# A decoder layer's opening stage: SyncE gets an ordered list, x gets five buffers, and ScalarE takes the first norm's variances

## The chip, the cores and the metric

The kernel runs on one core of a Trainium2 chip. The metric is the time of one execution on the device in microseconds; the time given for a kernel is the median of its runs.

## The reference

A decoder layer with three post-norm blocks over x of 8 batches, 256 tokens and 512 features (B, S, D). `LN` is a layer norm without gain and bias.

```
# 1: linear attention, head width 128 (M: 128x128, z: 128, a scalar gate)
q, k, v = x @ w_q.T, x @ w_k.T, x @ w_v.T;  sq, sk = elu(q)+1, elu(k)+1
mem   = (sq @ M) / (sq @ z + eps)
local = (sum over s' <= s of (sq[s] . sk[s']) v[s']) / (same sum of sq[s] . sk[s'] + eps)
x1 = LN(x + (g * mem + (1 - g) * local) @ w_o.T),   g = sigmoid(gate)
# 2: ctx is k and v, x1 is q; per 8x8 head a causal convolution over 512 features
kv[i,j] = k[i] * v[j];  y = conv(kv[i,j], ssm_kernel[h]) + D[h] * kv[i,j]
x2 = LN(x1 + sum over i of y[i,j] * q[i])
# 3: gated FFN (width 1408) with 4-bit weights and a scale per group of 128
h = silu(x2 @ Wg.T) * (x2 @ Wu.T);  f = h @ Wd.T
out = LN(x2 + f / rms(f))
```

## The kernel before

**Two parts.** `first_stage` is everything up to the first group; `periods` is the regular part. Blocks 2 and 3 go in 8 groups g of 32 tokens of every batch (256 rows of x). In period `it` the engines do the convolution of group `it` and, beside it, the FFN of group `it - 1`. Period 1 and all of block 1 (the attention) and of the conversion of the weights are one opening, written out by hand: each engine walks a list, `START_PE`, `START_DVE`, `START_ACT`, `START_POOL`. A step with `+` belongs to period 1, one without to the first stage. Then come period 2, a loop over periods 3 to 6, period 7 and a last FFN, each by the fixed lists `PE_ORDER`, `DVE_ORDER`, `ACT_ORDER`, `POOL_ORDER` and their `LAST_` forms. Engines meet only at semaphores, and each engine takes its steps strictly in the order of its list; so a step that waits holds up all that stand behind it.

**The attention** goes over 8 slots i of two batches by 128 tokens: slots 0 to 3 hold tokens 0 to 127, slots 4 to 7 tokens 128 to 255. So groups 0 to 3 read only slots 0 to 3. One slot, by the steps' names (PE steps are capital letters): the x rows land in `ring[i % 3]`; `Xa Xb` transpose them, `xa xb` (ScalarE) keep them; `Q` and `V` project, `re` (ScalarE) and `sg` (VectorE) make elu+1, `vk` keeps v; `S` scores, `mk` masks, `M` and `N` fill `p_n0`, `p_n1`, `dn` inverts the denominators, `lc` (ScalarE) and `o` (VectorE) combine, `T` transposes, `ok` keeps, `Oa Ob` project into `p_n0`, `p_n1`, and `ra rb` add x, in place in the ring buffer. Then `bn` (`statistics`: bn_stats and bn_aggr per half, and adding eps, on VectorE), `pw` (GpSimd, power -1/2), `nb` (VectorE, the shift -mean * rs), `nm` (ScalarE, two Identity activations in place), and SyncE stores the slot to `x1_rows` in HBM. A buffer is loaded anew only after its store has landed.

**The weights.** `u0` to `u4` (VectorE) unpack 4-bit codes, `ws0` to `ws32` (GpSimd) scale them, `w` (PE) transposes, `wh` (ScalarE) and `wl` (VectorE) keep high and low halves. `sk` writes the convolution kernel into `kpad`.

**The convolution.** `rv` (ScalarE, `reverse_ctx`) reads the context rows in `cnat[p]`, `f` or `+ct` (PE) transposes them, `kt` keeps, `pr` (GpSimd) makes products, `hk` (ScalarE) and `kl` (VectorE) split them, `c0` to `c15` convolve with the Toeplitz tiles `toe[p]`, `tm` multiplies by q, `tr` sums, `q`/`+qt` transposes q from `xq[p]`, `kq` keeps it, `rt`, `bq`, `pq`, `nq`, `xt`, `xh`, `xl` finish x2. A `+d0` is the convolution step 0 of the next group. In the FFN `g3_1` is tile 3, scale group 1, of gate and up; `rs3_1` (ScalarE) rescales the sum before `g3_2` may go on; `gu`, `hh`, `hl` make h; `y0_5` is tile 5 of the down projection of row half 0; `n0`, `a0`, `b0`, `e0` end a half. `tl` touches Silu, so that its table is loaded.

**SyncE** issues every DMA, on one queue. Its order before is program text, not a list: the weights and x slots 0 to 2, the Toeplitz rows written and read back, then for each slot its store and the load three slots on, with other loads after stores 3 to 6. Period 1's loads (`body(1, late=False)`) follow the last of the stores:

```
        for i in range(SLOTS):
            store_x1(i)
            if i + 3 < SLOTS:
                load_x(i + 3)
```

`ACT_ORDER`, which is not changed, opens each period with `rv0 tl rs0_1`: the reversal of the context rows of the next group, then the first rescale.

Of the kernel before, what the change touches and what calls it, by code (L numbers as in the profile page):

```python
# [12 lines left out]
P = 128  # L13
# [13 lines left out]
GT = 2  # L27
# [8 lines left out]

LATE = ("y1", "n1", "a1", "b1", "e1")
# [278 lines left out]
def first_stage(nc, sb, sem, keep, cv, bank, x, ctx_in, wq, wk, wv, wo, gate, M, z, ssm, ssm_d, gu_packed, gu_scales,  # L316
# [31 lines left out]
    ring = [sb(f"ring{k}", [P, 2, D], F32) for k in range(3)]  # L348
# [23 lines left out]
    in_x = [sem(f"in_x{k}") for k in range(3)]  # L372
    x1_stored = [sem(f"x1_stored{k}") for k in range(3)]
# [11 lines left out]
    o_flipped, oT_kept, proj_done, z_made = sem("o_flipped"), sem("oT_kept"), sem("proj_done"), sem("z_made")  # L385
    stats, rs_made, shifted, x1_made = sem("stats"), sem("rs_made"), sem("shifted"), sem("x1_made")
# [15 lines left out]
    def on_sync(sp):  # L402
        rows = bass.AP(toeplitz_rows.tensor, 0, [[4 * 640, 16], [1, P], [640, 4], [1, D]])

        def load_x(i):
            wait(sp, x1_stored[i % 3], 16 * (i // 3))
            sp.dma_start(ring[i % 3][:], tokens(x, i)).then_inc(in_x[i % 3], 16)

        def store_x1(i):
            sp.wait_ge(x1_made, 2 * i + 2)  # L410
            sp.dma_start(tokens(x1_rows, i), ring[i % 3][:]).then_inc(x1_stored[i % 3], 16)
# [31 lines left out]
        sp.wait_ge(kernel_split, 4)  # L443
        sp.dma_start(toeplitz_rows, kpad[:]).then_inc(rows_stored, 16)
        for p in range(2):
            sp.wait_ge(cv.ctx_reversed, p + 1)
            load_ctx(1, p)
        sp.wait_ge(rows_stored, 16)
        sp.wait_ge(wts_flipped, 4)
        for p in range(2):  # L450
            load_toe(0, p)
        for i in range(SLOTS):
            store_x1(i)
            if i + 3 < SLOTS:
                load_x(i + 3)
            if i == 3:

                sp.wait_ge(x1_stored[0], 32)
                for k in (1, 2):
                    sp.wait_ge(x1_stored[k], 16)  # L460
                for p in range(2):
                    load_rows(cv.xq, cv.in_xq, 0, p)
                for p in range(2):
                    load_rows(cv.xr, cv.in_xr, 0, p)
            if i == 4:
                sp.wait_ge(cv.ctx_reversed, 3)
# [12 lines left out]
        for k in range(3):
            sp.wait_ge(x1_stored[k], 16 * ((SLOTS - 1 - k) // 3 + 1))  # L480

    def on_pool(pool):
# [59 lines left out]
    def on_scalar(act):  # L542
# [105 lines left out]
    def on_vector(dve):  # L648
# [126 lines left out]
        def residual(i, e):  # L775
            dve.wait_ge(proj_done, 2 * i + e + 1)
            r = ring[i % 3][:, e, :]
            nc.vector.tensor_tensor(r, (p_n0, p_n1)[e][:], r, ALU.add).then_inc(z_made, 1)

        def statistics(i):  # L780
            for e in range(2):
                dve.wait_ge(z_made, 2 * i + e + 1)
                nc.vector.bn_stats(st[:, i, e, :], ring[i % 3][:, e, :]).then_inc(stats, 1)
            for e in range(2):
                dve.wait_ge(stats, i * 5 + e + 1)
                dve.sem_inc(cv.seen, 1)
# [16 lines left out]
        def step(s):  # L803
# [47 lines left out]
    def on_tensor(pe, flips):  # L851
# [20 lines left out]
        def flip_x(i, half):  # L872
            pe.wait_ge(in_x[i % 3], 16 * (i // 3 + 1))
# [3 lines left out]
            for k in range(2):  # L877
                for e in range(2):
                    done = flip(p_x[:, (k * 2 + e) * P:(k * 2 + e + 1) * P],
                                ring[i % 3][:, e, (2 * half + k) * P:(2 * half + k + 1) * P])  # L880
# [119 lines left out]
    free = [(sq_made, SLOTS), (xT_kept, 2 * SLOTS), (oT_kept, SLOTS), (z_made, 2 * SLOTS)]  # L1000
# [3 lines left out]
def periods(nc, sb, sem, keep, cv, bank, free, ctx_in, toeplitz_rows, x1_rows, out):  # L1004
# [30 lines left out]
    def on_sync(sp):  # L1035
# [34 lines left out]
        body(1, late=False)  # L1070
# [44 lines left out]
    def on_scalar(act):  # L1115
# [65 lines left out]
    def on_vector(dve):  # L1181
# [134 lines left out]
def decoder_layer(nc, x, ctx_2048, w_q, w_k, w_v, w_o, gate, M, z, ssm_kernel, ssm_d, gu_packed, gu_scales,  # L1316
# [3 lines left out]
    START_PE = ("iw0 Xa0 iw1 iz0 iw2 Xb0 iw3 Q0 V0 Xa1 S0 w0 M0 w1 f0 Xb1 w2 N0 w3 Q1 w4 T0 Xa2 w5 Oa0 w6 Ob0 f1 w7 "  # L1320
# [148 lines left out]
```

## Time and profile before

| what | value |
|---|---|
| median of 3 runs | 579.14 us (578.35 to 579.87) |
| the profiled execution | 574.02 us, span 572.3 us from first to last instruction |
| busy share of the span | PE 92%, ScalarE 72%, VectorE 67%, GpSimd 68% |
| mean granted TensorE clock | 0.984 of 2.4 GHz |

Rows give start and length in us. An engine's idle time stands in brackets, with what ended it; "issue" is idle time for which the profile shows no releaser. PE instructions overlap, so a row's length is longer than its distance to the next row. `PEld` is the weight load. `SPq` is SyncE's issue of a DMA: its length is that of the issue, not of the transfer. Lines are those of the kernel printed above.

### The profile page before, as it was taken

What the parts mean: (1) busy time and instruction counts of PE and PEld (TensorE: products, weight loads), DVE (VectorE), ACT (ScalarE), POOL (GpSimd) and SP (SyncE); (2) the same over time, 40 slices, a digit from 0 to 9 for tenths busy, and PEclk for the clock granted to TensorE, in tenths of its full rate; (3) what the DMA queues carried; (4) which work ended last, traced back from release to release, by engine and by line L of the source; (5) the groups of instructions that cost most, each with busy time, mean ns of one, the idle gap of its engine ahead of it and who ended that gap; (6) DMA issues with size and microseconds to landing.
All of it is one profiled execution on the core that took longest, in us unless ns stands there. A gap on an engine that the chain in (4) does not pass through costs nothing.

```text
span 572.3 us, 11933 instructions
## 1 busy us (share of the span) xinstructions
PE 526.1 (92%) x3798; PEld 396.7 (69%) x3798; DVE 383.4 (67%) x1153; ACT 414.4 (72%) x978; POOL 388.8 (68%) x449
## 2 busy tenths in 40 slices
PE   5897997996999799999999999999999999998992
PEld 4686785875777467767876777687678767765660
DVE  3984665877776457787777768767877777763223
ACT  3474672535789568878897898788778968887980
POOL 2896762596287538976996798499769967972231
PEclk9998998999999899999999999999999999999997
DMA  9214233403022513012210311040121102001001
GB/s 234 74 52 140 74 115 107 129 1 92 2 75 88 133 50 98 3 57 77 89 47 11 110 55 55 20 145 0 55 81 65 37 0 75 2 1 37 2 19 37
DMA packets 26594, 36.44 MB, mean 64 GB/s; under 512 B 4474, under 2 KB 13818, under 8 KB 26554
## 3 DMA queue, kind: packets, MB, share of 16 engines
q1 hardware_dynamic: 26554, 35.94, 20.8%
q8 instruction: 21, 0.34, 0.3%
q14 instruction: 19, 0.16, 0.1%
HBM read 27.46 MB, written 8.47 MB: 63 GB/s over the span
## 4 chain that ended last, share of the span: by engine, by line
PE 78%; ACT 6%; DVE 6%; DMA 4%; issue 4%; SPq 1%; POOL 1%; POOLq 0%; DVEq 0%; ACTq 0%
PE p_cv L141 7%; PE p_cv L143 7%; PE p_cv L142 7%; PE p_n L1277 6%; PE p_n L1279 6%; PE p_n L1278 6%; PE p_qk L1264 5%; PE p_qk L1266 5%; PE p_x L1264 5%; PE p_ct L99 4%; PE p_x L1266 4%; PE p_s L1266 3%; PE p_s L1264 3%; PE p_qk L890 3%; DMA x_rows<-ring 2%
## 5 line engine op out<-in xcount | busy, mean ns | idle before, releaser
L1122 ACT ACTIVATE p_qk<-p_qk,rescale 128x256 f32<-128x256 f32 x192 | 78.7, 454 | 27.5 <-PE p_qk L1266 27.2
L141 PE MATMUL p_cv<-kv_hi,toe 128*128 128x288 f16 x320 | 92.0, 287 | 6.5 <-issue 6.5
L143 PE MATMUL p_cv<-kv_hi,toe 128*128 128x288 f16 x320 | 92.1, 288 | 0.0
L142 PE MATMUL p_cv<-kv_lo,toe 128*128 128x288 f16 x320 | 92.0, 287 | 0.0
L1090 POOL TENSOR_TENSOR h_lo<-w,h_hi 128x256 f16<-128x256 f32 x88 | 59.4, 682 | 45.2 <-ACT h_hi L1139 44.6
L300 POOL TENSOR_TENSOR shared<-shared 128x1024 f32<-128x1024 f32 x32 | 75.5, 2360 | 16.7 <-DVE shared L260 16.6
L1122 ACT ACTIVATE p_x<-p_x,rescale 128x256 f32<-128x256 f32 x192 | 79.0, 458 | 6.2 <-PE p_x L1266 5.5
L1264 PE MATMUL p_qk<-x_hi,wg_hi 128*128 128x256 f16 x256 | 63.0, 273 | 6.3 <-ACT p_qk L1122 3.3
L226 DVE TENSOR_TENSOR kv_lo<-kv,kv_hi 128x1152 f16<-128x1152 f32 x32 | 60.5, 1889 | 11.6 <-ACT kv_hi L190 10.8
L1277 PE MATMUL p_n<-wd_hi,h_hi 128*128 128x512 f16 x176 | 67.0, 381 | 0.5 <-POOL h_lo L1090 0.5
L1278 PE MATMUL p_n<-wd_lo,h_hi 128*128 128x512 f16 x176 | 67.0, 380 | 0.0
L1279 PE MATMUL p_n<-wd_hi,h_lo 128*128 128x512 f16 x176 | 67.0, 380 | 0.0
L242 DVE TENSOR_TENSOR shared<-p_cv,qv 128x128 f32<-128x128 f32 x128 | 36.5, 285 | 44.3 <-PE p_cv L143 44.3
L1264 PE MATMUL p_x<-x_hi,wg_hi 128*128 128x256 f16 x256 | 63.1, 273 | 1.0 <-ACT p_x L1122 0.6
L1266 PE MATMUL p_x<-x_lo,wg_hi 128*128 128x256 f16 x256 | 62.9, 273 | 0.0
L1266 PE MATMUL p_qk<-x_lo,wg_hi 128*128 128x256 f16 x256 | 62.9, 273 | 0.0
L1122 ACT ACTIVATE p_s<-p_s,rescale 128x256 f32<-128x256 f32 x144 | 59.4, 461 | 2.7 <-PE p_s L1266 2.3
L207 POOL TENSOR_TENSOR kv<-kT 128x512 f32<-128x512 f32 x32 | 40.8, 1276 | 26.1 <-DVE kv_lo L226 26.1
L245 DVE TENSOR_TENSOR shared<-p_cv,qv 128x128 f32<-128x128 f32 x128 | 49.6, 388 | 0.0
L302 POOL TENSOR_TENSOR shared<-shared 128x512 f32<-128x512 f32 x32 | 47.9, 1497 | 2.5
L1266 PE MATMUL p_s<-x_lo,wg_hi 128*128 128x256 f16 x192 | 47.5, 274 | 0.0
L1264 PE MATMUL p_s<-x_hi,wg_hi 128*128 128x256 f16 x192 | 47.5, 274 | 0.0
(162 smaller groups left out, 1300.0 us busy)
## 6 DMA issues: line engine op xcount, KB each, us to landing
toe<-toeplitz_rows SPq DMA_DIRECT2D x16, 512.0 KB, 3.7
ring<-in_x SPq DMA_DIRECT2D x8, 512.0 KB, 3.8
cnat<-in_ctx SPq DMA_DIRECT2D x16, 256.0 KB
x_rows<-ring SPq DMA_DIRECT2D x8, 512.0 KB, 2.8
xq<-x_rows SPq DMA_DIRECT2D x16, 256.0 KB
xr<-x_rows SPq DMA_DIRECT2D x16, 256.0 KB
out_x<-fin SPq DMA_DIRECT2D x16, 256.0 KB
shared<-in_L_ffn_gate_up_packed SPq DMA_DIRECT2D x1, 704.0 KB, 6.9
```

Of the source, the lines that this page charges most:

```text
L141: nc.tensor.matmul(dst, hi, kh, start=(mb == 0), stop=False)
L142: nc.tensor.matmul(dst, hi, kl, start=False, stop=False)
L143: done = nc.tensor.matmul(dst, lo, kh, start=False, stop=(mb == lb))
L226: nc.vector.tensor_tensor(cv.kv_lo[h % 2][:], cv.kv32[:], cv.kv_hi[h % 2][:], ALU.subtract).then_inc(cv.kv_low, 1)
L300: nc.gpsimd.tensor_tensor(T[:, :, 0:256], T[:, :, 0:256], T[:, :, 256:512], ALU.add).then_inc(cv.tree, 1)
L1090: nc.gpsimd.tensor_tensor(h_lo[:, i, :], h32[:, i % 2, :], h_hi[:, i, :], ALU.subtract).then_inc(h_low, 1)
L1122: done = nc.scalar.activation(sums, sums, ACT.Copy, scale=rescale[:, p - 1, part * GI + i:part * GI + i + 1])
L1264: nc.tensor.matmul(dst, whi, cv.x2_hi[:, k, :], start=(k == 0 and part == 0), stop=False, skip_group_check=True)
L1266: done = nc.tensor.matmul(dst, whi, cv.x2_lo[:, k, :], start=False, stop=True, skip_group_check=True)
L1277: nc.tensor.matmul(p_y[t][:], h_hi[:, i, c], wd_hi[:, i, :], start=(i == 0), stop=False)
L1278: nc.tensor.matmul(p_y[t][:], h_hi[:, i, c], wd_lo[:, i, :], start=False, stop=False)
L1279: done = nc.tensor.matmul(p_y[t][:], h_lo[:, i, c], wd_hi[:, i, :], start=False, stop=(i == GI - 1))
```

## The change

SyncE gets a list of its own, `START_SYNC`, for what follows the load of x slot 2, and period 1's loads are in it. `x3` loads slot 3, `st0` stores slot 0, `tw` writes the Toeplitz rows, `toe4` loads Toeplitz tile p = 0 of group 2 (number = 2g + p), `cx6` the context rows of group 3, p = 0, and `xq`, `xr` likewise. x gets five buffers, the two new ones being `z3` and `fin`, which the FFN uses from group 0 on; `sq` becomes scratch of the attention too. `bn_stats` and `bn_aggr` go from the attention: `ra rb` now also sum a row (`accum_out`), `bm` makes the negative mean, `qs` (ScalarE, two Square activations with bias and `accum_out`) sums the squared deviations, `bn` scales and adds eps, and `nb` multiplies. The four other opening lists are new orders. The order of the regular periods is not touched.

```
-    ring = [sb(f"ring{k}", [P, 2, D], F32) for k in range(3)]
+    ring = [sb(f"ring{k}", [P, 2, D], F32) for k in range(3)] + [keep["z3"], keep["fin"]]
...
-            pool.wait_ge(stats, i * 5 + 5)
+            pool.wait_ge(stats, i + 1)
...
+        def deviations(i):
+            act.wait_ge(mean_made, i + 1)
+            for e in range(2):
+                nc.scalar.activation(sq[:, e], ring[i % RING][:, e, :], ACT.Square, bias=negmean[:, i, e:e + 1],
+                                     accum_out=dev[:, i, e:e + 1]).then_inc(deviated, 1)
...
-            nc.vector.tensor_tensor(r, (p_n0, p_n1)[e][:], r, ALU.add).then_inc(z_made, 1)
-
-        def statistics(i):
...
+            nc.vector.scalar_tensor_tensor(out=r, in0=(p_n0, p_n1)[e][:], scalar=1.0, in1=r, op0=ALU.mult, op1=ALU.add,
+                                           accum_out=total[:, i, e:e + 1]).then_inc(z_made, 1)
...
-        body(1, late=False)
+        store(0, 0)
...
+    START_SYNC = ("cx2 x3 x4 st0 x5 tw0 st1 x6 st2 st3 toe0 xq0 xr0 xq1 xq2 cx3 xr1 toe1 toe2 cx5 x7 st4 xq4 xq3 cx4 "
+                  "toe3 xr2 xr3 toe4 xq5 st5 toe5 st6 st7 cx7 cx6").split()
-    START_PE = ("iw0 Xa0 iw1 iz0 iw2 Xb0 iw3 Q0 V0 Xa1 S0 w0 M0 w1 f0 Xb1 w2 N0 w3 Q1 w4 T0 Xa2 w5 Oa0 w6 Ob0 f1 w7 "
+    START_PE = ("Xa0 iw0 Xb0 iw1 iw2 iw3 iz0 Q0 V0 Xa1 S0 M0 N0 Xb1 Q1 w0 T0 f0 w1 Oa0 Ob0 w2 w3 S1 Xa2 w4 V1 w5 Xb2 "
+                "M1 N1 Q2 T1 w6 w7 Oa1 Ob1 Xa3 w8 V2 w9 S2 M2 Xb3 N2 w10 w11 Q3 T2 f1 w12 w13 Oa2 Ob2 Xa4 w14 w15 V3 "
...
+                "w28 Xa6 Oa4 Ob4 w29 w30 V5 w31 w32 q0 S5 M5 c0 Xb6 c1 q1 c2 c3 N5 c4 Q6 c5 c6 T5 c7 Oa5 f2 c8 Ob5 c9 "
+                "S6 c10 c11 f3 V6 c12 c13 Xa7 M6 rt0 c14 Xb7 c15 q2 N6 Q7 +c0 q3 T6 +c1 rt1 Oa6 Ob6 +c2 xt0 V7 xt1 S7 "
...
+                "+g10_2 +d1 +y0_6 +g10_3 +xt0 +y0_7 +y0_8 +y0_9 +xt1 +y0_10").split()
-    START_DVE = ("is0 fs0 u0 sg0 u1 mk0 ig0 dn0 u2 o0 u3 ra0 sg1 rb0 bn0 mk1 sk0 nb0 dn1 kl0 o1 ra1 rb1 sg2 kl1 mk2 "
+    START_DVE = ("is0 fs0 sg0 mk0 ig0 dn0 u0 o0 u1 sg1 ra0 rb0 mk1 u2 dn1 o1 bm0 kl0 ra1 rb1 sg2 bn0 mk2 dn2 bm1 nb0 "
...
+    START_ACT = ("xa0 kw0 xb0 kw1 ks0 kw2 kw3 ge0 re0 vk0 xa1 xb1 rv0 lc0 ok0 wh0 re1 wh1 kt0 wh2 rv1 wh3 xa2 vk1 xb2 "
...
+                 "wh25 nm2 xb5 nm3 lc4 wh26 wh27 ok4 wh28 re5 wh29 wh30 kt1 wh31 wh32 vk5 xa6 kq0 qs4 xb6 hk2 lc5 kq1 "
...
+                 "+gu10 +xt0 +hh10 qs7 +xt1 +n0 nm5 nm6 nm7").split()
```

Before, `nm5`, `nm6` and `nm7` stand among the earlier steps of `START_ACT`, `nm7` after `+rs7_1`, and the list ends with `+hh10 +xt0 +n0 +xt1`; `START_PE` ends with `+y0_8 +y0_9 +y0_10 +xt1`.

## Rows read from the trace of the kernel before

**Rows 1.** The page, part 1: busy time, share of the span, instructions.

```profile
PE 526.1 (92%) x3798; PEld 396.7 (69%) x3798; DVE 383.4 (67%) x1153; ACT 414.4 (72%) x978; POOL 388.8 (68%) x449
```

**Rows 2.** Windows, all engines: stretch, length, busy time of each, PE clock, DMA share, GB/s.

```profile
5.30:203.20 197.90, 175.05 (x1185) 140.58 (x1186) 134.91 (x404) 116.01 (x243) 124.39 (x149) 0.97 0.31 90
...
149.20:203.20 54.00, 47.99 (x357) 35.56 (x356) 32.70 (x111) 43.69 (x106) 34.79 (x35) 0.97 0.28 79
...
203.20:209.10 5.90, 4.69 (x30) 2.53 (x28) 4.50 (x11) 2.83 (x9) 3.10 (x5) 1.00 0.02 4
209.10:500.00 290.90, 288.42 (x2196) 216.03 (x2195) 216.77 (x673) 244.72 (x596) 233.42 (x248) 1.00 0.18 56
```

**Rows 3.** Timeline of PE: the three longest waits after the start.

```profile
52.67 1.11 PE L856 MATMUL p_x<-ident,ring 128*128 128x128 f32 x4 [3.33 <-DMA ring<-in_x]
...
89.45 0.66 PE L99 MATMUL p_ct<-ident,xq 128*128 128x128 f32 x4 [2.47 <-DMA xq<-x_rows]
...
192.14 0.28 PE L141 MATMUL p_cv<-kv_hi,toe 128*128 128x288 f16 x1 [3.96 <-issue]
```

**Rows 4.** Timeline of SyncE's DMA issues.

```profile
48.41 0.37 SPq L407 DMA_DIRECT2D ring<-in_x  x1
...
81.17 0.38 SPq L411 DMA_DIRECT2D x_rows<-ring  x1
83.97 0.37 SPq L407 DMA_DIRECT2D ring<-in_x  x1
...
177.75 0.38 SPq L411 DMA_DIRECT2D x_rows<-ring  x1
180.56 0.62 SPq L1046 DMA_DIRECT2D xq<-x_rows  x1
...
183.12 0.48 SPq L1043 DMA_DIRECT2D toe<-toeplitz_rows  x1
```

**Rows 5.** Window right behind the first of those waits, columns as in rows 2.

```profile
52.50:55.90 3.40, 3.23 (x15) 3.23 (x16) 0.00 (x0) 1.56 (x3) 1.11 (x2) 0.50 0.00 0
```

**Rows 6.** Timeline of PE: the steps `Q2` and `Oa1 Ob1`.

```profile
39.28 3.62 PE L890 MATMUL p_qk<-xT,wT 128*128 128x256 f32 x16
...
43.58 1.98 PE L946 MATMUL p_n<-woT,oT 128*128 128x512 f32 x4
```

**Rows 7.** Groups by line and shape: one slot's statistics, and their nearest likenesses.

```profile
L783 DVE BATCH_NORM_STATS2 st<-ring 128x6 f32<-128x512 f32 x16 | 10.2, 678 | 0.0
...
L608 ACT ACTIVATE ring<-ring,shift,rs 128x512 f32<-128x512 f32 x16 | 12.2, 813 | 0.0
```

**Rows 8.** Timeline of ScalarE: a table load, and the end of the opening.

```profile
138.08 1.28 ACT L1154 ACT_TABLE_LOAD   x1
...
202.93 0.60 ACT L1148 ACTIVATE sq<-p_n 128x512 f32<-128x512 f32 x1 [1.20 <-PE p_n L1279]
...
203.51 0.58 ACT L194 CAST x_hi<-p_ct 128x512 f16<-128x512 f32 x1
203.98 0.63 ACT L178 COPY crev<-cnat 128x512 f32<-128x512 f32 x1
...
207.78 0.81 ACT L1122 ACTIVATE p_qk<-p_qk,rescale 128x256 f32<-128x256 f32 x2 [3.07 <-PE p_qk L1266]
```

**Rows 9.** Timeline of POOL: the first scaled weights, and the last.

```profile
15.93 6.33 POOL L516 TENSOR_TENSOR w<-shared,sc_g 128x256 f32<-128x256 fp8e4 x8 [11.38 <-DVE shared L731]
...
83.26 2.33 POOL L516 TENSOR_TENSOR w<-shared,sc_d 128x256 f32<-128x256 fp8e4 x4 [0.44 <-PE p_cv L856]
```

**Rows 10.** Waits of PE from 5.3 to 203.2: total us, times, longest us.

```profile
PE p_cv L856 <- POOL w L516: 2.5, 3, 1.1
```

**Rows 11.** Windows of one us: what the DMA engines moved, columns as in rows 2.

```profile
82.00:83.00 1.00, 0.90 (x9) 0.74 (x8) 1.00 (x3) 0.39 (x2) 0.82 (x2) 1.00 0.93 354
...
188.00:189.00 1.00, 0.18 (x2) 0.00 (x0) 0.97 (x2) 1.00 (x3) 0.92 (x2) 1.00 1.12 210
```

**Rows 12.** Timeline of PE at the same place.

```profile
207.13 0.28 PE L1264 MATMUL p_qk<-x_hi,wg_hi 128*128 128x256 f16 x1 [1.21 <-DVE x_lo L288]
```

More of the change, by code:

```diff
@@ L371, in first_stage @@
     in_sc, in_pg, in_pd, in_k = sem("in_sc"), sem("in_pg"), sem("in_pd"), sem("in_k")
-    in_x = [sem(f"in_x{k}") for k in range(3)]
-    x1_stored = [sem(f"x1_stored{k}") for k in range(3)]
+    in_x = [sem(f"in_x{k}") for k in range(RING)]
+    x1_stored = [sem(f"x1_stored{k}") for k in range(RING)]
     ident_made, masks_made, ones_made, consts = sem("ident_made"), sem("masks_made"), sem("ones_made"), sem("consts")
@@ L400, in tile, with on_sync @@
         return ("g", n) if n < OG else ("d", n - OG)
[L402 removed]
+    def on_sync(sp, order):
         rows = bass.AP(toeplitz_rows.tensor, 0, [[4 * 640, 16], [1, P], [640, 4], [1, D]])
         def load_x(i):
[L406 to L407 removed]
+            wait(sp, x1_stored[i % RING], 16 * (i // RING))
+            sp.dma_start(ring[i % RING][:], tokens(x, i)).then_inc(in_x[i % RING], 16)
         def store_x1(i):
             sp.wait_ge(x1_made, 2 * i + 2)
[L411 removed]
+            sp.dma_start(tokens(x1_rows, i), ring[i % RING][:]).then_inc(x1_stored[i % RING], 16)
         def load_ctx(g, p):
@@ L479, in on_sync, with step @@
-        for k in range(3):
-            sp.wait_ge(x1_stored[k], 16 * ((SLOTS - 1 - k) // 3 + 1))
+        def step(s):
+            name, i = named(s)
+            g, p = i // 2, i % 2
+            if name == "x":
+                load_x(i)
+            elif name == "st":
+                store_x1(i)
+            elif name == "tw":
+                sp.wait_ge(kernel_split, 4)
+                sp.dma_start(toeplitz_rows, kpad[:]).then_inc(rows_stored, 16)
+            elif name == "cx":
+                sp.wait_ge(cv.ctx_reversed, i - 1)
+                load_ctx(g, p)
+            elif name == "toe":
+                if g == 0:
+                    sp.wait_ge(rows_stored, 16)
+                    sp.wait_ge(wts_flipped, 4)
+                else:
+                    sp.wait_ge(cv.convolved, 8 * (i - 1))
+                load_toe(g, p)
+            else:
+                for k in range(4):
+                    sp.wait_ge(x1_stored[k], 16)
+                if name == "xq":
+                    if g > 0:
+                        sp.wait_ge(cv.q_flipped, i - 1)
+                    load_rows(cv.xq, cv.in_xq, g, p)
+                else:
+                    if g > 0:
+                        sp.wait_ge(cv.x2_summed, i - 1)
+                    load_rows(cv.xr, cv.in_xr, g, p)
@@ L482, in on_pool @@
+        for s in order:
+            step(s)
+        for i in range(4, SLOTS):
+            sp.wait_ge(x1_stored[i % RING], 16 * (i // RING + 1))
     def on_pool(pool):
@@ L879, in flip_x @@
                     done = flip(p_x[:, (k * 2 + e) * P:(k * 2 + e + 1) * P],
-                                ring[i % 3][:, e, (2 * half + k) * P:(2 * half + k + 1) * P])
+                                ring[i % RING][:, e, (2 * half + k) * P:(2 * half + k + 1) * P])
             done.then_inc(x_flipped, 1)
@@ L1147, in square @@
             act.wait_ge(y_done[t], f + 1)
+            if isinstance(f, int) and f == 0:
+                act.wait_ge(*free[6])
             nc.scalar.activation(sq[:, t], p_y[t][:], ACT.Square, accum_out=ss[:, t]).then_inc(y_squared[t], 1)
@@ L1200, in add_residual @@
             dve.wait_ge(cv.x2_held[t], f + 1)
+            if isinstance(f, int) and f == 0:
+                dve.wait_ge(*free[4])
             nc.vector.scalar_tensor_tensor(out=z3[:, t, :], in0=p_y[t][:], scalar=rr[:, t], in1=x2hold[:, t, :],
@@ L1213, in finish @@
             wait(dve, stored[t], f * 16)
+            if isinstance(f, int) and f == 0:
+                dve.wait_ge(*free[5])
             nc.vector.tensor_scalar(fin[:, t, :], z3[:, t, :], mv3[:, t, 0:1], rs3[:, t], ALU.subtract,
@@ L1420, in _ @@
             def _(sp):
-                first[0](sp)
+                first[0](sp, START_SYNC)
                 rest[0](sp)
```

95 lines of the change are left out of this document (32 added, 63 removed), and 38 rows, old and new, of tables (START_ACT, START_DVE, START_PE).

## The prediction

> **What bounds the kernel now.** I read the page first, then windows over long stretches, then the waits and timelines of PE and SyncE where a window shows PE idle. The page says PE is busy 92% of the span [rows 1]. The windows say where the other 8% lies: in the regular part PE is busy 288.42 of 290.90 us, in the opening 175.05 of 197.90 [rows 2]. So the regular part, which keeps its orders, is bound by PE and has 2.5 us to give in those 291; the opening has 197.90 - 175.05 = 22.85 us of idle PE after its first instruction. Whatever is won or lost at the seam between the two is carried to the end, since PE behind it has no slack to catch up with.
>
> The timeline of PE puts 3.33 + 2.47 + 3.96 = 9.76 us of it in three waits [rows 3]. The first is the load of x slot 3: it was issued at 48.41, behind a store that had to free the buffer, and PE got it at 52.67 [rows 3, 4]. The second is the first q rows, which need the stores of slots 0 to 3; the last of these was issued at 81.17, SyncE moved on at 83.97, and the rows landed at 89.45. The third is put down to "issue", but the step is `+d0`, whose Toeplitz tile was issued only at 183.12, behind the store at 177.75, which SyncE had to see landed at 180.56 before it began period 1's loads [rows 4]. PE restarted at half clock after each of the three: the window behind the first has the clock at 0.50 for 3.4 us (1.2 instead of 2.4 GHz), the windows behind the two others look the same, three in all, and the opening as a whole shows 0.97 [rows 2, 5]. PE is busy in them, so each costs 3.4 x 0.5 = 1.7 us of work beyond the idle time. The three waits together are worth 9.76 + 5.1 = 14.9 us. The remaining 13.1 us is some twenty gaps of 0.1 to 1.5 us.
>
> **The change, part by part.**
>
> *Buffers and SyncE's list.* `x3` and `x4` now wait for no store, only for `cx2`, which stands before them and waits for the first context reversal, before 20 us here. They land long before `Xa3`: the first wait goes, 3.33 + 1.7. For `q0`, `nm3` runs right after `xb5`. From `Xb5` to `q0` the new PE list has some 11.5 us of work (`Q5` 3.5 and `Oa4 Ob4` 1.8, a little under the rows' lengths as instructions overlap [rows 6]; by the same timeline `N4` 0.9, `V5` 1.8, seven `w` of 0.44, `T4` and `Xa6` 0.7). Against it stand `xb5` 0.6, `nm3` 1.5, and the way from store to rows landed, 89.45 - 81.17 = 8.3 us [rows 4], or 10.4, and up to 2 us more for the Toeplitz load that now sits between them. Nearly even: I take this wait as gone, bounds 0 to 2 us left. `toe4` is issued after the step `+c7`, long before `+d0`: the third wait goes. Sum -14.9, bounds -11 and -14.9. In return `x7`, with `st4` behind it, is queued after `toe2`, which waits for `c7`, and after `cx5`, which waits for `rv3`; from `c7` to `Xa7` PE has some 10 us of work, the chain (`f2` 1.4, ScalarE's `hk3 kt2 rv3` 2.4, two issues, a load of 4.3 as in 52.67 - 48.41) takes 9 [rows 3, 4]. I cost it at nothing; uncovered it is up to 3 us.
>
> *Statistics.* VectorE loses per slot two bn_stats of 0.68 us and three small ones, and gains two small ones [rows 7]; about 1.4 us x 8 = 11 us off it. ScalarE gains two Squares. The one Square of the trace, with its accumulator read, delays the next instruction by 203.51 - 202.93 = 0.58 us [rows 8]; the nearest of this source, the Identity of `nm`, takes 0.81 [rows 7]. So 1.2 to 1.6 per slot, 10 to 13 us in all, on an engine busy 116 of 198 us here [rows 2]. Neither engine sets PE's pace before 149 us. After it ScalarE is near full (43.69 of 54.00) [rows 2], but there `nm6` and `nm7` leave its middle (3 us) while `qs7` comes in near the end, so it is no worse. Net on PE: 0, bounds -1 and +2.
>
> *New orders.* `u0` now stands behind slot 0's `dn0`. GpSimd's scaling of weights, which begins at 15.93 [rows 9], then begins near 21.4: `sg0` ends at about 15.6, `mk0 ig0 dn0` need till 19.1, `u0` takes 2.3. A tile takes 6.33 / 4 = 1.6 us at first and 2.33 / 2 = 1.2 later [rows 9]; with `pr0`, `pr1` and the roots all 33 are done near 74 to 80. PE, which has more attention ahead of them, wants the last at about 83. So the late start costs only in `w0` to `w3`, some 1.6 us, against 2.5 before [rows 10]. Two other gaps (slot 0's `M0` behind a late `vk0`; `rt1` behind `kq3`) have longer covers in the new lists. Of the 13.1 us of small gaps I take 10 to be left: -3, bounds -7 and +5, since twenty gaps between five new lists can't be followed one by one.
>
> *The seam.* Here I expect a new wait. `START_ACT` ends `+n0 nm5 nm6 nm7`; `ACT_ORDER` goes on `rv0 tl rs0_1`. This `rv0` reads what `cx6` loads, and `cx6` is the last of SyncE's list, behind `st7`, which waits for `nm7`. Count from T, where `y0_10` ends and PE's opening is over. `n0` takes ScalarE to T + 0.7, the three `nm` of 2 x 0.7 to T + 4.9. SyncE issues `st5` at T + 2.3, `toe5`, `st6`, `st7` at T + 5.1, `cx7`, and `cx6` at about T + 6.2. Alone it would land 3.5 us on, at T + 9.7. But it has 2.4 MB of stores, Toeplitz tile and context ahead of it, and the DMA engines move 354 GB/s of a store and 210 when Toeplitz and row loads are among it [rows 11]: 1.6 MB / 354 + 1.0 MB / 210 = 4.4 + 5.0 = 9.4 us from T + 3.2, T + 12.6. The load at 183.12, with 1 MB ahead of it, needed nine us till PE had it [rows 3, 4], so a queue in order of issue is what this trace shows. I take T + 12.5, bounds T + 9.7 and T + 14. Then `rv0`, `tl` and `rs0_1` take 0.5 + 0.1 + 0.8 [rows 8], and `g0_1` can start at T + 13.9. Till there PE has 4.6 us of work (4.69 busy between 203.2, where the opening ended, and 209.1, where `g0_1` began [rows 2]); it waits 9.3 us and restarts at half clock, 1.7. Against this the 1.3 us of idle at this place now goes, as `xl1` comes ahead of `b0` [rows 2, 12]. Sum +9.7, bounds +7 and +11.3.
>
> The Trainium skill speaks to this (DMA: Bandwidth & Descriptors, "Queues, rings and completion order"): each DMA engine takes the descriptors of one ring in order, so a late load queues behind all that SyncE issued before it. By it the landing is T + 12.6 rather than the T + 9.7 of a load alone; the 183.12 row agrees.
>
> **The sum.** -14.9 + 0 - 3 + 9.7 = -8.2 us. The profiled execution took 574.02 (span 572.3, 1.7 around it), which gives 565.8. It is 5.1 us under the median of the runs, and nothing in the sum scales with the difference: 579.14 - 8.2 = 570.9 us.
>
> **The rivals.**
>
> *The seam costs little* (0.15). If the stores and loads share the engines so that `cx6` lands near T + 9.7, and the small gaps halve, the sum is -14.9 - 6.5 + 7 = -14.4: 565. For it: a store alone lands in 2.8 us [rows 4]. Against: six transfers are issued within 4 us.
>
> *The orders leave as much idle time as they take* (0.14). With the small gaps unchanged and `x7` late by 3 us, with its restart at half clock, the sum is -8.2 + 3 + 4.7 = -0.5: 578.6, no change. If the q rows are late by 2 us as well, with their restart, it is +3.2: 582.3, slower; it decides from the point where such waits exceed 10 us in all. For it: SyncE's list has two loads that PE needs behind waits for PE's own progress. Against: both chains are covered by my count, if barely.
>
> *Square brings its table with it* (0.06). Slots 0 to 4 need Exp between the Squares. In the trace Square runs beside Silu without a load, and Relu, Copy and Identity beside Exp; Square beside Exp is not in it. If each of the five `qs` before `tl` loaded a table and the next `re` another, 1.28 us each as the load for Silu [rows 8], that were 13 us on ScalarE, in front of steps that PE waits for (`wh`, `re`, `ok`): with all of it on PE the sum is -8.2 + 13 = +4.8, 583.9, slower. It decides once more than 10 us of the 13 reach PE.
> The Trainium skill (ScalarE: Activation LUTs, "Table sets: the hidden batching unit") names relu, copy, identity and abs as the functions that every set holds, and square not; by it this rival would come true. The trace shows Square without a load only beside Silu, so I leave it at a small chance.
>
> **The numbers.** The forecast has 0.65: 570.9, its own range 565 to 577 from the bounds above (-8.2, less 5, plus 6). Over all cases 563.5 to 578.5 leaves about 2 in 10 outside. Measured runs of this kernel can tell 0.3%, 1.7 us, from no change. Faster: the first case but for its last twentieth, the second, and a little of the third, 0.80; same 0.09; slower 0.11.
>
> **What would show it.** PE's waits on `ring<-in_x` and before `+d0` are gone, and that on `xq` is under 2 us; the opening ends (T) near 185 instead of 203.2. No ACT_TABLE_LOAD but the two. Right behind T ScalarE idles some 7 us before `crev` L178, released by the DMA of `cnat`, PE some 9 us before L1264 of `p_qk`, and a window behind it has the clock at 0.50. From there the rest takes as long as now. I am wrong if `crev` is released within 4 us of `nm7`, if T lies above 195, or if the clock drops at new places in the opening.

## The result, and the profile after

The changed kernel takes 560.86 us (median of 4 runs, 558.73 to 561.49), the kernel before 578.75 beside it (577.38 to 579.87): ratio 0.9685, 95% interval 0.9651 to 0.972. The sign of the forecast is right, the size is not: 570.9 with a range of 563.5 to 578.5 was forecast. The profiled execution took 561.49 us (span 559.8). The ratios given can differ a little from the quotient of two medians; two executions of before in a later comparison, at 582.2 and 583.0 us, are counted as slow and left out of them.

The page, part 1, of the changed kernel, to be read against [rows 1]:

```profile
PE 523.8 (94%) x3798; PEld 396.7 (71%) x3798; DVE 381.3 (68%) x1145; ACT 425.0 (76%) x1010; POOL 387.8 (69%) x449
```

VectorE lost 2.1 us, ScalarE gained 10.6 us, PE is busy 2.3 us less for the same 3798 instructions. Only some 0.5 us of that is less time at half clock: by windows of one microsecond half clock cost PE 4.9 us of work in the trace of before and 4.4 in this one. Windows of the changed kernel, columns as in [rows 2]: the opening, what is left of it, the wait behind it, what follows the wait, and the regular part.

```profile
4.40:177.60 173.20, 168.59 (x1185) 139.06 (x1186) 132.76 (x396) 122.82 (x270) 123.75 (x150) 1.00 0.32 90
177.60:182.20 4.60, 4.50 (x27) 2.45 (x25) 3.08 (x8) 4.60 (x8) 1.90 (x4) 1.00 0.35 111
182.20:192.30 10.10, 0.03 (x1) 0.03 (x2) 2.80 (x11) 1.81 (x6) 2.48 (x4) 0.76 0.75 240
192.30:197.70 5.40, 5.40 (x20) 3.06 (x21) 0.00 (x0) 3.00 (x9) 0.00 (x0) 0.50 0.48 185
197.70:490.00 292.30, 289.83 (x2214) 217.43 (x2213) 218.32 (x675) 245.26 (x597) 235.49 (x250) 1.00 0.16 51
```

The opening now holds 173.20 - 168.59 = 4.61 us of idle PE, against 22.85, and its clock is 1.00, against 0.97. Then come ten microseconds in which PE does nothing and 5.4 at half clock (1.2 of 2.4 GHz). The regular part again has 2.5 us of idle time in some 292. Behind it, at 504.7, PE runs 3.7 us at half clock, where the trace of before has full clock; that costs 1.7 us (the row stands in the last section). All the idle time of PE up to 200 us by the chain of its waits, what it waited for, and on the right total, count and longest:

```profile
PE p_qk L1280 <- ACT p_qk L1132: 10.2, 1, 10.2
PE p_x L866 <- DMA ring<-in_x: 4.5, 1, 4.5
PE p_cv L142 <- DVE kv_lo L227: 2.1, 1, 2.1
PE p_cv L866 <- POOL w L518: 0.8, 2, 0.5
PE p_qk L900 <- ACT xT L567: 0.7, 1, 0.7
PE p_x L866 <- ACT xT L567: 0.4, 1, 0.4
PE p_cv L142 <- DVE shared L261: 0.2, 1, 0.2
```

The wait of 4.5 is the start; before, it was 5.3, since the old list began with the weights and the new one begins with `Xa0`. None of the three waits of [rows 3] is there, and of the some twenty small gaps six are left. The first row is the new wait. The timeline of SyncE shows why the old ones went:

```profile
21.57 0.47 SPq L409 DMA_DIRECT2D fin<-in_x  x1
...
103.24 0.46 SPq L409 DMA_DIRECT2D ring<-in_x  x1
...
144.83 0.37 SPq L420 DMA_DIRECT2D toe<-toeplitz_rows  x1
...
179.71 0.39 SPq L413 DMA_DIRECT2D x_rows<-ring  x1
180.14 0.47 SPq L420 DMA_DIRECT2D toe<-toeplitz_rows  x1
181.12 1.79 SPq L413 DMA_DIRECT2D x_rows<-ring  x2
182.97 1.86 SPq L416 DMA_DIRECT2D cnat<-in_ctx  x2
```

The loads of slots 3 and 4 are issued by 22 us, where slot 3 had to wait till 48.41, and the Toeplitz tile of `+d0` is issued at 144.83 instead of 183.12 [rows 4]. The last four rows are `st5`, `toe5`, `st6 st7`, `cx7 cx6`: the queue of the seam. Timeline of ScalarE and then of PE there:

```profile
178.18 4.33 ACT L616 ACTIVATE ring<-ring,shift,rs 128x512 f32<-128x512 f32 x6
190.80 0.62 ACT L179 COPY crev<-cnat 128x512 f32<-128x512 f32 x1 [8.29 <-DMA cnat<-in_ctx]
```

```profile
192.28 0.40 PE L1280 MATMUL p_qk<-x_hi,wg_hi 128*128 128x256 f16 x1 [10.17 <-ACT p_qk L1132]
```

ScalarE is done with `nm7` at 182.51 and waits 8.29 us for the rows of `cx6`; the rescale that PE needs stands behind that reversal. PE loses 10.17 us to it, where before it lost 1.21 [rows 12].

### The profile page after: what moved, and what is told of

It reads as the page before. It is cut to its first block, busy times and chain, and to the rows that moved or that the text cites. A ratio compares the mean times of both kernels' runs of the same rounds, so it can differ in the third digit from the quotient of the medians.

```text
span 559.8 us, 11973 instructions
## 1 busy us (share of the span) xinstructions
PE 523.8 (94%) x3798; PEld 396.7 (71%) x3798; DVE 381.3 (68%) x1145; ACT 425.0 (76%) x1010; POOL 387.8 (69%) x449
## 4 chain that ended last, share of the span: by engine, by line
PE 85%; ACT 4%; DVE 3%; issue 3%; POOL 2%; DMA 2%; SPq 0%; POOLq 0%; DVEq 0%; ACTq 0%
PE p_cv L142 7%; PE p_cv L144 7%; PE p_cv L143 7%; PE p_n L1293 6%; PE p_n L1294 6%; PE p_n L1295 6%; PE p_qk L1280 5%; PE p_qk L1282 5%; PE p_ct L100 5%; PE p_x L1280 5%; PE p_x L1282 5%; PE p_s L1282 3%; PE p_s L1280 3%; PE p_qk L900 3%; PE p_n L911 2%
## 5 line engine op out<-in xcount | busy, mean ns | idle before, releaser
L1280 PE MATMUL p_qk<-x_hi,wg_hi 128*128 128x256 f16 x256 | 63.9, 276 | 15.2 <-ACT p_qk L1132 13.4
L227 DVE TENSOR_TENSOR kv_lo<-kv,kv_hi 128x1152 f16<-128x1152 f32 x32 | 59.2, 1849 | 20.5 <-ACT kv_hi L191 19.8
```

Of the source, the lines that this page charges most:

```text
L227: nc.vector.tensor_tensor(cv.kv_lo[h % 2][:], cv.kv32[:], cv.kv_hi[h % 2][:], ALU.subtract).then_inc(cv.kv_low, 1)
L1280: nc.tensor.matmul(dst, whi, cv.x2_hi[:, k, :], start=(k == 0 and part == 0), stop=False, skip_group_check=True)
```

## The experiments

**The seam.** The first four kernels shared their 13 runs of before (median 577.46). The first asks whether the seam is the late context load. Edit of the changed kernel:

```
-                  "toe3 xr2 xr3 toe4 xq5 st5 toe5 st6 st7 cx7 cx6").split()
+                  "toe3 xr2 xr3 toe4 xq5 cx6 cx7 st5 toe5 st6 st7").split()
```

> The changed kernel with cx6 and cx7 issued right after xq5, ahead of st5, in SyncE's list; nothing else. Theory (the seam waits for cx6, which is queued behind st5, toe5, st6, st7 and cx7): crev L179 no longer waits for a DMA, PE's wait of 10.17 us before the first p_qk matmul behind the seam falls to about 2 us (nm5, nm6, nm7 still stand ahead of rv0: T + 0.7 + 4.3 + 0.6 + 0.1 + 0.8 = T + 6.5 against 4.6 us of PE work), and the 5.4 us at half clock behind it go. 10.2 - 1.9 + 2.7 = 11 us faster than the changed kernel: about 550. Rival (the wait comes from the three nm themselves, or the regular part has slack and takes the loss back): under 4 us faster, 557 to 561.

Measured: 549.44 us (548.68 to 550.2), ratio 0.9549 (0.9488 to 0.961). Its timelines of ScalarE and PE:

```profile
179.56 4.33 ACT L616 ACTIVATE ring<-ring,shift,rs 128x512 f32<-128x512 f32 x6
183.80 0.61 ACT L179 COPY crev<-cnat 128x512 f32<-128x512 f32 x1
```

```profile
185.25 0.28 PE L1280 MATMUL p_qk<-x_hi,wg_hi 128*128 128x256 f16 x1 [1.76 <-ACT p_qk L1132]
```

The reversal now follows `nm7` at once, and PE waits 1.76 us instead of 10.17. Two steps of one list were worth 11.4 us: the seam's wait is the place of `cx6` in SyncE's queue, and not the work of ScalarE ahead of it.

**Statistics.** The changed kernel with the statistics on VectorE again (`bn_stats` in the place of `bm`, `bn_aggr` in that of `bn`, no `qs`), lists and buffers kept:

```
-            nc.vector.tensor_scalar(negmean[:, i, :], total[:, i, :], -1.0 / D, None, ALU.mult).then_inc(mean_made, 1)
+            for e in range(2):
+                dve.wait_ge(z_made, 2 * i + e + 1)
+                nc.vector.bn_stats(st[:, i, e, :], ring[i % RING][:, e, :]).then_inc(mean_made, 1)
```

> The changed kernel with bn_stats and bn_aggr on VectorE again (bn_stats at the places of bm, bn_aggr and eps at those of bn), no Squares on ScalarE, residual without a row sum; all lists, buffers and SyncE's list kept. Theory A (the statistics were no matter to PE; the orders closed the gaps): within 1.5 us of the changed kernel, 559.5 to 562.5. Theory B (VectorE was what made the small gaps of the opening, and 11 us less on it closed them): the small gaps come back in part, the opening ends 3 to 8 us later, 564 to 569.

Measured: 561.6 us (559.99 to 562.9), ratio 0.9756 (0.9691 to 0.982). That is 0.7 us above the changed kernel, inside the spread of either. PE's waits in its profile are those of the changed kernel, with 10.5 us at the seam. The two pages give what the change of statistics moves by itself: VectorE is busy 386.2 us here and 381.3 in the changed kernel, ScalarE 414.3 and 425.0.

**Buffers alone.** The kernel before with five x buffers and nothing else:

```
-            if i + 3 < SLOTS:
-                load_x(i + 3)
+            if i + 5 < SLOTS:
+                load_x(i + 5)
```

> The kernel before with five x buffers (slots 3 and 4 loaded right after slot 2, slot i + 5 after the store of slot i), its lists and statistics kept. By the prediction's own term the wait of 3.33 us for x slot 3 and its window at half clock go, 5.0 us: about 573.7 against 578.75 of before. Rival (the small gaps behind it grow by as much, since VectorE and GpSimd used the pause to catch up): 577 to 579.

Measured: 570.87 us (567.89 to 573.32), ratio 0.9891 (0.9849 to 0.9932), 6.6 us. The wait for slot 3 is gone, that for the q rows is 1.3 us instead of 2.5. Two waits that the profile of before didn't have stand at 23.10 (0.98, for the mask) and 30.60 (1.93, for `o`). They are not the work of the buffers: the next kernel but one, which keeps three, has the same two. The rows are under "Single moves".

**The changed kernel again**, in the same group, to tie the times together.

> The changed kernel once more, beside the others on the same chip: 560.9 within 0.3%. It gives its spans and clocks beside those of before, whose profiled execution was 4.7 us under its timed runs: if that was a difference between executions of before, its runs here scatter between 574 and 580 while this kernel's stay within 2 us.

Measured: 560.86 us (559.13 to 561.91), ratio 0.9742 (0.9673 to 0.9811).

**Loads alone.** The kernel before with period 1's loads ahead of the stores of slots 5, 6 and 7 in SyncE's program (the four other lists as before):

```
+            if i == SLOTS - 1:
+                for p in range(2):
+                    sp.wait_ge(cv.q_flipped, p + 3)
+                    load_rows(cv.xq, cv.in_xq, 2, p)
...
+                sp.wait_ge(cv.convolved, 24)
+                load_toe(2, 0)
```

> The kernel before with only SyncE's program altered: the loads of Toeplitz rows and context for groups 1 to 3 and of the rows of x1 for group 2 stand ahead of the stores of slots 5, 6 and 7 instead of behind them (toe 2 and 3 at slots 5 and 6, toe4, cx6, xq4, xq5, xr2, xr3 at slot 7); three buffers, lists and statistics as before. Theory (three PE waits that the profile puts down to issue, 1.45, 1.13 and 3.96 us, are these loads held up behind stores): all three go and with the last of them its window at half clock, 6.5 + 1.7 = 8.2 us: about 569 against 577.5. Rival (the two short ones are no waits for a load, since they were among the small gaps of my prediction): only 5.7 us, 572.

Measured: 567.36 us (566.08 to 568.82), ratio 0.9804 (0.9767 to 0.984), 11.1 us under its own before (578.49). That is 2.9 more than the theory's 8.2. All three waits put down to `toe` loads are gone.

**Both, without the new orders and statistics.**

> Five buffers and the early loads together in the kernel before, its lists and statistics kept. If the waits are independent, the two gains add: 5 to 6.6 (five buffers alone ran at 570.9 against 577.5) and 8.2, so 563 to 564. What is then left to the changed kernel without its seam wait (549.4) is the work of the four new orders alone: 14 us. Rival: they overlap, 567 or more.

Measured: 560.3 us (559.0 to 562.09), ratio 0.9694 (0.9657 to 0.9731), 18.2 us under before. By the medians buffers and loads add up (6.6 + 11.1 = 17.7), and by themselves they give as much as the whole change does. By the profiled executions they don't add so neatly (574.0 before; 570.7, 568.8 and, with both, 559.9): the profiles of the two single kernels have a half-clock window at 31 us that those of before and of this kernel lack. PE's longest waits up to 200 us in its profile:

```profile
PE p_qk L867 <- DMA toe<-in_L_attn_w_q: 5.3, 1, 5.3
PE p_cv L867 <- POOL w L527: 2.5, 3, 1.1
PE p_n L936 <- issue: 2.0, 2, 1.0
PE p_ct L99 <- DMA xq<-x_rows: 1.6, 1, 1.6
PE p_ct L99 <- ACT qv L184: 1.5, 1, 1.5
...
```

Behind the start (5.3) stand the short waits of the old orders, which the new ones don't have, and what is left of the wait for the q rows: 1.6 us, with a window at half clock behind it. So ctx_early (549.4: everything but the seam) against this kernel (560.3) gives the worth of the new orders with the statistics: 10.9 us. The two ran in different comparisons. Pairs of one comparison give 8.6 (the next kernel, 551.7, against this one) and 11.8 (550.1 against 561.9, among the single moves, each kernel one move away from these).

**The norms out of the opening.** The kernel with the early context, and `nm5`, `nm6`, `nm7` behind `gu1`, `gu2`, `gu3` of period 2 instead of ahead of its first step:

```
-                 "+gu10 +xt0 +hh10 qs7 +xt1 +n0 nm5 nm6 nm7").split()
+                 "+gu10 +xt0 +hh10 qs7 +xt1 +n0").split()
```

> The kernel with cx6 and cx7 early, and nm5, nm6, nm7 taken out of the end of ScalarE's opening and put behind gu1, gu2 and gu3 of period 2. Theory (the 1.8 us that PE still waits at the seam are these 4.3 us of ScalarE's): that wait goes, 547.5 against 549.4. Rival (PE is bound by ScalarE's rescales behind the seam, so what is moved in comes back there): 549 to 551.

Measured: 551.66 us (550.68 to 552.89), ratio 0.9542 (0.9509 to 0.9574), the same ratio as with the early context alone; the theory's 547.5 did not come. The 1.76 us at the seam went, waits of the same size came elsewhere (1.5 for `p_x`, 1.0 for the q rows).

**The kernel before against itself.**

> The kernel before once more, beside the others. Its runs scattered from 571.6 to 583.0, those of the changed kernel by 3 us. Theory (the long waits of PE for DMAs each may or may not bring windows at half clock, and their landing times vary): granted clock and span of its executions go together, 0.98 at 572 and 0.96 or less at 583. Rival (the scatter is of another kind): the clock is the same in all.

Measured: 576.17 us (574.65 to 581.07), ratio 0.9982 (0.9954 to 1.001). Its executions differ in the granted clock (0.984 to 0.976) as well as in time, and the two go together: in all comparisons the kernel before took 571.6 us at 0.987, 573.9 to 575.2 at 0.984 or 0.982, and 579.0 to 580.1 at 0.976.

**Single moves.** The last four ask which moves of the new orders bring the 10.9 us; their before was 577.87. First a wait that the change left, at 120.60 in the kernel with the early context: VectorE's `kl4` is put ahead of `dn6 bm5 nq0`.

```
-                 "... mk6 tm12 tm13 bq0 tm14 tm15 dn6 bm5 nq0 kl4 "
+                 "... mk6 tm12 tm13 bq0 tm14 tm15 kl4 dn6 bm5 nq0 "
```

> The early-context kernel (549.4 us) with VectorE's kl4 moved ahead of dn6 bm5 nq0. In its profile PE waits 2.12 us at 120.6 for kv_lo and restarts at half clock. Theory (in the opening every microsecond of PE's idle time reaches the end, and a wait of 2 us or more costs 1.7 us more by the clock): the wait falls to under 0.5 us, the half-clock window behind it goes, 549.4 - 1.6 to 3.8, so 545.6 to 547.8. Rival (nq0, and with it x2hold and the first half of x2, come 1.9 us later and the wait only moves): 549 to 550.

Measured: 551.27 us (549.65 to 553.71), ratio 0.9546 (0.95 to 0.9592); not faster. Timeline of PE without the move, and with it:

```profile
120.60 0.30 PE L142 MATMUL p_cv<-kv_hi,toe 128*128 128x288 f16 x1 [2.12 <-DVE kv_lo L227]
...
121.17 0.76 PE L100 MATMUL p_ct<-ident,xq 128*128 128x128 f32 x4
```

```profile
118.76 0.30 PE L142 MATMUL p_cv<-kv_hi,toe 128*128 128x288 f16 x1
...
121.41 0.66 PE L100 MATMUL p_ct<-ident,xq 128*128 128x128 f32 x4 [2.10 <-DMA xq<-x_rows]
```

`+c0` starts 1.84 us earlier, and then `q3` waits for rows that land only at 121.4. That load was hidden behind the wait for `kv_lo`. SyncE issued it right after `xq4`, the two from 114.58 on, after a pause since 103.81: `xq4` waits for `q2` to have been transposed (the transposes start at 113.89), and `xq3` stands behind it. A gap of 0.72 us, for `o`, came too.

Next, `u0` back ahead of slot 0's `sg0`:

```
-    START_DVE = ("is0 fs0 sg0 mk0 ig0 dn0 u0 o0 ...
+    START_DVE = ("is0 fs0 u0 sg0 mk0 ig0 dn0 o0 ...
```

> The early-context kernel with VectorE's unpacking u0 put back in front of slot 0's sg0. Theory A (the late start of GpSimd's scaling costs nothing, what PE gains is that sg0, mk0 and dn0 of slot 0 no longer stand behind an unpacking): sg0 is 2.3 us later, PE waits some 2 us more for slot 0's S0 or M0, 551 to 552. Rival (the weights are what PE waits for at 24 and 27 us): those two waits of 0.5 and 0.3 go and nothing else comes, 548.6 to 549.4.

Measured: 550.14 us (548.29 to 551.1), ratio 0.952 (0.9476 to 0.9564); no difference. PE's two waits for `w` (0.8) are gone, and this one came:

```profile
16.82 0.71 PE L924 MATMUL p_s<-sqk 128*128 128x128 f32 x4 [1.44 <-DVE sqk L747]
```

Then two moves of the new orders made in the kernel with old orders, five buffers and early loads: `vk0` ahead of `rv0` on ScalarE, and with it, in a second kernel, `u1` and `u2` behind `dn0` and `o0` on VectorE.

```
-    START_DVE = ("is0 fs0 u0 sg0 u1 mk0 ig0 dn0 u2 o0 u3 ...
+    START_DVE = ("is0 fs0 u0 sg0 mk0 ig0 dn0 u1 o0 u2 u3 ...
...
-    START_ACT = ("kw0 xa0 kw1 ks0 xb0 kw2 ge0 kw3 re0 rv0 vk0 xa1 ...
+    START_ACT = ("kw0 xa0 kw1 ks0 xb0 kw2 ge0 kw3 re0 vk0 rv0 xa1 ...
```

> The old orders with five buffers and the early loads (560.3 us), with ScalarE's vk0 ahead of rv0. In the profile of the old orders ScalarE waits 2.25 us for context rows in front of rv0, vk0 stands behind it, and PE waits 1.0 us in front of slot 0's M0. Theory (a short gap of PE is worth its own length): 559.3. Rival (the steps behind are bound by VectorE's unpacking, the gap only moves to N0 or to the weights): 560.3.

> The same, and also VectorE's u1 behind dn0 and u2 behind o0, so that slot 0's mask, denominators and combination no longer stand behind an unpacking. Theory (the new lists close the gaps of the first 50 us by this): PE's waits for the mask, o and ring there (about 0.9, 0.4, 0.4) go too, together with vk0 some 2.5 us, 557.5 to 558.5. Rival (GpSimd's weights come later by as much, since ws has no code to scale): PE's wait for w grows from 2.5 by 1 to 2 us, 559 to 561.

Measured: 561.89 us (559.6 to 563.01), ratio 0.9716 (0.9669 to 0.9763), and 562.15 us (560.29 to 563.46), ratio 0.972 (0.9675 to 0.9765). Neither is faster than 560.3. PE's timeline without a move (first fence), with `vk0` first (second) and with all three moves (third):

```profile
10.65 3.72 PE L901 MATMUL p_qk<-xT,wT 128*128 128x256 f32 x16 [0.24 <-ACT xT L576]
...
18.92 0.68 PE L936 MATMUL p_n<-Mz,sqk 128*128 128x129 f32 x4 [1.01 <-issue]
...
27.30 0.66 PE L867 MATMUL p_cv<-ident,w 128*128 128x128 f32 x4 [1.03 <-POOL w L527]
...
28.37 0.44 PE L867 MATMUL p_s<-ident,o 128*128 128x128 f32 x2 [0.41 <-DVE o L781]
```

```profile
22.86 0.71 PE L945 MATMUL p_n<-vext,AT 128*128 128x129 f32 x4 [0.98 <-DVE AT L760]
...
27.78 0.66 PE L867 MATMUL p_cv<-ident,w 128*128 128x128 f32 x4 [0.31 <-POOL w L527]
...
30.36 0.54 PE L867 MATMUL p_s<-ident,o 128*128 128x128 f32 x2 [1.93 <-DVE o L781]
```

```profile
27.09 0.66 PE L867 MATMUL p_cv<-ident,w 128*128 128x128 f32 x4 [1.03 <-POOL w L527]
...
28.16 0.44 PE L867 MATMUL p_s<-ident,o 128*128 128x128 f32 x2 [0.41 <-DVE o L781]
...
32.87 0.97 PE L867 MATMUL p_cv<-ident,w 128*128 128x128 f32 x4 [2.39 <-POOL w L527]
```

The second fence invites the reading that `vk0` took the 1.01 us away and that the mask and `o` took its place. It does not hold, for the kernel with the early loads alone, which has no move at all, shows the same:

```profile
11.80 5.06 PE L900 MATMUL p_qk<-xT,wT 128*128 128x256 f32 x16
...
23.30 0.71 PE L944 MATMUL p_n<-vext,AT 128*128 128x129 f32 x4 [0.98 <-DVE AT L759]
...
30.80 0.44 PE L866 MATMUL p_s<-ident,o 128*128 128x128 f32 x2 [1.93 <-DVE o L780]
```

What these executions share is a slower start of PE. Slot 0's `Q`, 3.72 us long and begun at 10.65 in the first fence, takes 5.06 from 11.80 with the early loads, 5.10 from 11.56 with five buffers alone, 4.46 from 11.95 with `vk0` first and 3.82 from 12.35 with the three moves. The transposes before it take 1.06 us, against 0.60, at a granted clock that the windows give as 1.00 in all of them. What makes a start slow was not found; no edit of these kernels touches PE's list. So the profiles can't say what the moves did to the first 30 us, and only the times count: neither is faster. With `u1` and `u2` moved back, the wait for `w` at 32.87 is 2.39; without a move it is 0.40, at 33.42. The new `START_PE` has `N0`, `Xb1` and `Q1` ahead of `w0`; that this is what makes the new orders work there is a guess, since no run moved PE's steps alone.

## Why the forecast was too small

Between kernels of neighbouring composition the runs split the change as follows. The third column is a difference of two medians, good to about 1.5 us, the fourth one of two profiled executions (spans 572.3, 558.1, 548.4, 559.8 us).

| term | forecast | medians | profiled | from |
|---|---|---|---|---|
| three long waits | -14.9 | -18.2 | -14.2 | both parts against before |
| new orders (small gaps), with the statistics | -3 | -10.9 | -9.7 | early context against both parts |
| of it the statistics | 0 | -0.7 | -1.4 | changed kernel against statistics back |
| seam | +9.7 | +11.4 | +11.4 | changed kernel against early context |
| sum | -8.2 | -17.7 | -12.5 | |

Two steps failed. Of the 10 us between 570.9 and 560.86, 4.3 lie in the sum itself: the small gaps gave 6.7 more than forecast, the seam cost 1.7 more and the three waits gave 0.7 less. Another 5.1 lie in the step from the sum to the median, and the last 0.6 is the changed kernel's profiled execution above its median.

*The three waits: mechanism right, size right.* All three went in the changed kernel, and `T`, the end of the opening, came to 177.4 where 185 was forecast. In the trace of before they hold 9.76 us of idle time and 4.9 of half clock. The kernel with both parts takes only two of them whole: it keeps 1.6 us and a window at half clock in front of the q rows. In exchange the early loads take two gaps that the forecast counted among the small ones: PE's timeline of before has 1.45 at 140.69 and 1.13 at 166.47, both in front of a convolution with a tile `toe` that SyncE had issued behind the stores of slots 5 and 6. Idle time of 3.3 + 4.0 + 0.9 + 2.6 and 3.3 of half clock make 14.1, which is the 14.2 of the profiled executions.

*The step to the median failed.* The sum was made against a profiled execution of 574.02 us and carried over to the median by adding 5.1: "nothing in the sum scales with the difference". The changed kernel has no such difference: its profiled execution, 561.49, lies 0.6 above its median. The runs show what sets the profiled execution of before apart. It had a mean clock of 0.984; most runs of before had 0.976 to 0.981, and the kernel with both parts has 0.987 to 0.993. From 0.984 to 0.979 over 577 us is an estimate of 2.9 us of the 4.7 to 5.1. The rise of the clock belongs to the gain. In which waits the typical execution of before loses it stays open; the second profile of before has one window at half clock more, at 138.5, behind a wait of 1.5 us that is none of the three.

*The small gaps: this step of the prediction failed.* "Of the 13.1 us of small gaps I take 10 to be left" was a guess in the middle of -7 and +5. In the profile 4.6 us were left. Counted by the stretches of the two traces, the opening, start included, is 203.2 - 177.6 = 25.6 us shorter: 14.7 are the three waits, 8.5 small gaps, 0.9 the earlier start, which the forecast didn't count, and 1.5 PE time that the clock doesn't explain. Against -14.9 - 3 that is 7.7 too little; the seam (11.5 instead of 9.7) and the half clock at 504.7 (1.6) hide 3.4 of it. I had named two gaps and left the rest at their old sum. The rows tell why that was poor: the new lists close a dozen gaps at once, and along with them a half-clock window (0.51 for 3.5 us behind the 1.6 us for the q rows that the old orders keep). Which of the moves carry the 10.9 us stays open; of those that were tried apart, `u0`, `vk0`, and `u1` and `u2` together with `vk0`, none gave a gain.

*The seam: right in place, cause and nearly in size.* `g0_1` was forecast at T + 13.9 with a wait of 9.3 and 1.7 us of half clock, and came at T + 14.9 with 10.17, and 5.4 x 0.5 = 2.7. `cx6` landed as if behind all that SyncE had queued: T + 13.4, with T + 12.6 worked out by the queue in order of issue and T + 9.7 for a load alone. By the Trainium skill's rule (DMA: Bandwidth & Descriptors, "Queues, rings and completion order") the former was to be expected, and the run that moves the load ahead of the stores bears it out with 11.4 us. The rival in which the seam costs little is refuted. The term was 1.8 us too small, 0.9 from the longer wait and 1.0 from the longer time at half clock.

*Statistics: right in the sum, wrong in one of its sizes.* Groups by line and shape of the changed kernel: the Identity, the Square, and the new mean on VectorE (the other new row there, `ve`, has 189 ns).

```profile
L616 ACT ACTIVATE ring<-ring,shift,rs 128x512 f32<-128x512 f32 x12 | 8.9, 810 | 1.0 <-DVE shift L802 1.0
...
L609 ACT ACTIVATE sq<-ring,negmean 128x512 f32<-128x512 f32 x12 | 8.5, 716 | 0.0
...
L793 DVE TENSOR_SCALAR negmean<-total 128x2 f32<-128x2 f32 x8 | 5.3, 657 | 0.0
```

ScalarE pays 10.6 us of busy time for all slots, 1.3 a slot, inside the forecast's 1.2 to 1.6. VectorE was to lose 11 us and lost about half of it: the four groups of the old statistics (10.2, 2.8, 2.1 and 1.7 us) make 16.8, the new ones (5.3, 1.5, 2.9, and 1.4 of read accumulators) 11.1, and the pages of the kernels with and without them differ by 4.9. An instruction on two columns took 657 ns in the mean (median 346, one of 2.3 us) and another 358, not 0.2 us. Neither engine's change reaches PE, as the run with the old statistics shows. No table load came with Square: the changed kernel has two, as before, although its Squares stand between Exp steps. So the rival of the table loads is refuted. The page behind it (the Trainium skill, ScalarE: Activation LUTs, "Table sets: the hidden batching unit") says less than the prediction took from it: it names four functions that every set holds, without Square, but leaves the lists of the sets open. It made the loads possible and not certain.

*`x7` behind PE's own progress* cost nothing: it was issued at 103.24, and no wait for x shows after the start. The same arrangement has its cost at another place, 11 us later, where `xq3` stands behind `xq4`; the wait for `kv_lo` hid it until that was taken away. The rival "orders leave as much idle time as they take" is refuted by 4.6 us left of 22.85. Of the signs of being wrong none came: `crev` was released 8.3 us after `nm7`, `T` lies below 195, and the clock drops nowhere in the opening.

The best version of all that ran is the changed kernel with `cx6 cx7` ahead of `st5`: 549.44 us, 0.9549 of before.

## What to carry to other kernels

When a queue gets its order by hand, look at what its last entries are and who reads them first: here moving two loads ahead of three stores gave back 11.4 us, two thirds of what the whole change had won. A wait in a profile ends with the last of several conditions; before it is priced, ask when the next one would have come, here the q rows came under 1 us after `kv_lo` (121.4 against 120.6), and none of the four kernels with a move or two of its own was faster, where reordering all lists gave about 11 us. Before a wait is laid to an edit, look for it in a kernel without that edit: the 1.93 us for `o` was there too. And if the profiled execution is not a typical one, ask which part of the difference the change itself takes away; here that was half of the forecast's miss.

## What the runs showed of the hardware

The price of a short wait in clock is not fixed. Windows behind the same wait for `kv_lo`, 2.12 us long in both kernels, first the changed kernel, then the one with the early context:

```profile
120.80:124.30 3.50, 3.41 (x22) 2.54 (x23) 3.07 (x11) 2.93 (x6) 2.78 (x4) 1.00 0.53 171
```

```profile
120.50:124.00 3.50, 3.38 (x17) 2.54 (x18) 2.12 (x9) 2.59 (x4) 2.78 (x4) 0.66 0.53 154
```

And behind the wait of 1.54 us for `x_lo` at 504.72 of two other kernels, the one with buffers and loads alone, and the changed one:

```profile
504.70:508.10 3.40, 3.38 (x24) 2.37 (x25) 2.51 (x6) 2.69 (x8) 0.65 (x2) 1.00 0.00 0
```

```profile
504.70:508.40 3.70, 3.68 (x16) 2.24 (x17) 2.65 (x6) 2.91 (x8) 0.61 (x2) 0.54 0.01 2
```

The kernel before shows it with no difference in the program, behind a wait of 1.5 and one of 0.5 us, in its first profile and in its second:

```profile
138.50:142.00 3.50, 2.05 (x14) 1.29 (x13) 2.02 (x9) 1.07 (x2) 2.50 (x4) 1.00 0.57 146
```

```profile
138.50:142.00 3.50, 3.01 (x10) 1.57 (x11) 2.17 (x8) 1.31 (x2) 2.25 (x3) 0.56 0.52 164
```

The same wait in front of the same work restarts at full clock in one execution and at about half in another. So a wait of 1.5 to 2 us costs between nothing and 1.7 us on top of its length. The times follow the clock: executions of before lay between 571.6 us at a mean clock of 0.987 and 580.1 at 0.976, but for two of 581.1 and 581.9 at 0.978 and 0.979, those of the changed kernel between 558.7 at 0.985 and 561.9 at 0.981. What decides between the two was not found.
